# The gate of the state-space layer: from VectorE, behind its scaled inputs, to GpSimd, behind its seventh addition

## The reference

```python
def _ssm(x, W_in, conv_w, dt_bias, A_log, D, norm_w, W_out):
    zxbcdt = x @ W_in.T
    z, xBC, dt_raw = ...                       # 512, 768 and 64 columns
    xBC = _causal_conv_silu(xBC, conv_w)       # -> xs, B, C
    dt = jax.nn.softplus(dt_raw + dt_bias)
    a = dt * -jnp.exp(A_log);  cum = jnp.cumsum(a)
    M = (C B^T) * exp(cum_i - cum_j), lower triangle, * dt_j
    y = M @ xs + D * xs                        # 128 positions x 512
    yz = y * (z * jax.nn.sigmoid(z))           # the gate
    yn = yz * jax.lax.rsqrt(jnp.mean(yz * yz, axis=-1) + EPS) * norm_w
    return yn @ W_out.T
```

## Time and profile before

| | |
|---|---|
| median of 3 runs | 2140.99 us (2137.66 to 2142.30) |
| the profiled execution | 2138.0 us, of which the span of the profile is 2136.1 |
| busy: TensorE, its weight loads | 1969.5 us (92% of the span), 1276.6 (60%) |
| busy: VectorE, ScalarE, GpSimd | 1627.4 (76%), 1378.5 (65%), 1230.6 (58%) |
| chain that ended last | PE 64%, DVE 16%, issue 7%, ACT 7%, POOL 5% |
| mean granted TensorE clock | 0.978 of full speed |

### The profile page before, as it was taken

One profiled execution on the slowest core, in us unless ns is written; L12 is line 12 of the kernel. 1 busy time (PEld: TensorE's weight loads), 2 busy tenths in 40 slices (PEclk: granted clock), 3 DMA queues, 4 the chain that ended last, 5 costly groups with the idle time before them and its releaser, 6 DMA issues.

```text
span 2136.1 us, 34822 instructions
## 1 busy us (share of the span) xinstructions
PE 1969.5 (92%) x9518; PEld 1276.6 (60%) x9620; DVE 1627.4 (76%) x3852; ACT 1378.5 (65%) x5262; POOL 1230.6 (58%) x1508
## 2 busy tenths in 40 slices
PE   7979999999999998799998848999999999999996
PEld 4636666666666666455554425666666666666664
DVE  7845676766776667689999846788888888787887
ACT  3555666666666666456663237777777777777774
POOL 0153445445545443377777825777777777777774
PEclk9989999999999999999999969999999999999999
DMA  6000000000000002100010020000000000000000
GB/s 229 1 18 6 3 4 3 2 2 5 2 2 2 2 0 85 69 1 30 21 31 10 1 74 16 4 4 6 6 6 6 6 8 6 6 5 6 3 3 8
DMA packets 30235, 37.56 MB, mean 18 GB/s; under 512 B 3472, under 2 KB 24464, under 8 KB 29456
## 3 DMA queue, kind: packets, MB, share of 16 engines
q1 hardware_dynamic: 30096, 36.11, 5.0%
HBM read 34.01 MB, written 2.10 MB: 17 GB/s over the span
## 4 chain that ended last, share of the span: by engine, by line
PE 64%; DVE 16%; issue 7%; ACT 7%; POOL 5%; DMA 0%; DVEq 0%; SPq 0%; POOLq 0%; ACTq 0%
PE xa_pS L755 5%; PE xa_pJB L736 5%; PE xa_pO L830 5%; PE xa_pY L867 5%; PE fa_pJB L1989 5%; PE xa_pJA L736 4%; PE fa_pS L2071 3%; PE ssm_pX L1434 3%; PE ssm_pL L1428 3%; PE fa_pO L2014 3%; PE fa_pY L2028 3%; PE fa_pJA L1969 2%; PE fa_pH L2120 2%; PE xa_pP L747 2%; POOL fa_rs L1919 2%
## 5 line engine op out<-in xcount | busy, mean ns | idle before, releaser
L2146 ACT ACTIVATE fa_qT<-fa_pH,all_fa_head_vec 128x512 f32<-128x512 f32 x128 | 99.6, 778 | 176.0 <-PE fa_pH L2120 176.0
L1919 POOL TENSOR_TENSOR fa_rs<-fa_rs,all_minus_half 128x4 f32<-128x4 f32 x192 | 197.9, 1031 | 15.0
L2155 ACT ACTIVATE fa_pS<-fa_pS,fa_nb 128x128 f32<-128x128 f32 x512 | 183.2, 394 | 6.8 <-issue 6.8
L1380 POOL TENSOR_TENSOR ssm_y<-ssm_y,ssm_term 128x512 f32<-128x512 f32 x112 | 145.8, 1302 | 60.9 <-DVE ssm_term L1677 39.6
L1916 POOL TENSOR_TENSOR fa_rs<-fa_ms,all_eps5w 128x4 f32<-128x4 f32 x192 | 44.4, 231 | 226.3 <-ACT fa_q_junk L2139 126.2
L2071 PEld LDWEIGHTS fa_pS<-fa_kT,fa_qT 128*128 128x128 f32 x1024 | 124.2, 191 | 65.5 <-ACT fa_qT L2146 58.6
L1944 POOL TENSOR_TENSOR fa_cat<-fa_ov,fa_om 128x512 bf16<-128x512 f32 x125 | 150.5, 1204 | 5.1
L2071 PE MATMUL fa_pS<-fa_kT,fa_qT 128*128 128x128 f32 x1024 | 148.2, 288 | 2.8 <-ACT fa_qT L2146 0.9
L1935 POOL TENSOR_TENSOR fa_ov<-fa_ob,fa_om 128x512 f32<-128x512 bf16 x125 | 144.4, 1156 | 0.9 <-DVE fa_om L2287 0.9
L682 POOL TENSOR_TENSOR xa_rs<-xa_ms,all_eps 128x4 f32<-128x4 f32 (+1 forms) x65 | 13.2, 203 | 225.1 <-ACT xa_junk L906 225.1
L924 ACT ACTIVATE xa_pr<-xa_pS,xa_nb,xa_rs 128x256 f32<-128x256 f32 x256 | 142.5, 568 | 0.2
(11 more groups left out here) (338 smaller groups left out, 5744.9 us busy)
## 6 DMA issues: line engine op xcount, KB each, us to landing
all_shared_weights<-in_fa_w SPq DMA_DIRECT2D x12, 512.0 KB, 3.7
fa_cat<-in_fa_wproj SPq DMA_DIRECT2D x8, 512.0 KB, 3.8
all_shared_weights<-in_xa_wq SPq DMA_DIRECT2D x1, 2048.0 KB, 13.8
xa_wo<-in_xa_wo SPq DMA_DIRECT2D x1, 2048.0 KB, 18.0
xa_ctxT<-in_ctxT SPq DMA_DIRECT2D x16, 128.0 KB, 2.1
all_shared_weights<-in_fa_wkvx SPq DMA_DIRECT2D x1, 2048.0 KB, 9.9
fa_ctxT<-in_ctxT SPq DMA_DIRECT2D x16, 128.0 KB, 2.1
out_x<-all_X SPq DMA_DIRECT2D x16, 128.0 KB, 1.7
```

The costliest lines, as they stand in the source:

```text
L1919: pool.tensor_tensor(rs[:, j % 2, cols], rs[:, j % 2, cols], env.mhalf[:, cols], ALU.pow)\
L2155: last = act.activation(four(pS[j % 2])[:, i, :], four(pS[j % 2])[:, i, :], ACT.Exp, bias=nb[:, j % 2, i:i + 1], accum_out=rsum[:, j % 2, ...
```

## The change

The gate moves from VectorE's list to GpSimd's. GpSimd now multiplies `y` of sequence m by `sz` in step m, right behind the seventh addition, and ahead of its scaled inputs for sequence m + 1. Before, VectorE did it in step m + 1, behind its own scaled inputs for sequence m + 1 (and behind the biased dt, in even steps). It waits for the seventh addition and for `sz`; TensorE's transposes and ScalarE's squares wait for the same semaphore (`gated`) as before.

```diff
@@ gpsimd, steps(m, ...), in "if attend:", behind the loop over the levels
                     if l == 2 and m > 2:
                         norm.pool_rstd(pool, m - 2, 0)
+                pool.wait_ge(y_added, now(m, 0, LEVELS, LEVELS - 1))
+                pool.wait_ge(s["z_in"], now(m, 0))
+                pool.tensor_tensor(y[:, side, :], y[:, side, :], sz[:, side, :], ALU.mult).then_inc(s["gated"], 1)
             elif back:
@@ vector, steps(m, ...)
             if paired and not first:
                 biased_dt(dve, m + 1)
-            if back:
-                dve.wait_ge(y_added, now(m - 1, 0, LEVELS, LEVELS - 1))
-                dve.tensor_tensor(y[:, 1 - side, :], y[:, 1 - side, :], sz[:, 1 - side, :], ALU.mult)\
-                    .then_inc(s["gated"], 1)
             terms(0, 1)
```

## The result

| | before | after |
|---|---|---|
| median of 5 runs | 2140.99 us (2137.66 to 2142.53) | 2150.35 us (2146.87 to 2152.52) |
| span of the profiled execution | 2136.1 us | 2145.1 us |
| first xdt of the stage to the last transpose | 341.8 us | 350.5 us |

The ratio is 1.0045, 95% interval 1.0033 to 1.0057: slower by 0.45%; between the medians lie 9.4 us, against 8.5 forecast. Of the 9.0 us between the two spans 8.7 lie in the state-space stage. Of all the executions reported here one, of the filled kernel before, took 7800.83 us; no profile shows why, and it is left out of that kernel's ratio.

A forecast was written before the change was run, and what follows sets the result against it. Bound: at even entries the path over VectorE's xdt and L1270, with GpSimd holding VectorE up. Pair costs, clock losses and the end sum to 8.7 us, taken as 8.5 over 2141.0: 2149.5 us, range 2139.5 to 2158.

The forecast's parts named there:

- The held xdt: VectorE's xdt, issued 0.18 us into GpSimd's gate, ends 0.55 us behind it: about 1.6 us in place of 0.68.
- Rival 1: At the entries xdt gets through unheld: even ones gain some 0.75 us, 6 us less in all, 2135; chance 0.08.
- The even entry, +0.2: Start of an even step: level 0 starts 0.96 us later, but the step loses 0.2 us at full clock.
- The odd entry, +0.34: Start of an odd step: GpSimd's scaled inputs end later, so y's first part (L1690) ends 0.34 us later.
- Rival 2: VectorE, rid of its gate, makes good the delay before the step's end: about +1.5 us, 2142.5; chance 0.2.
- Rival 3: Behind xdt GpSimd's scaled input starts before VectorE's, adding 1.07 us per entry: 15 more, about 2165; chance 0.03.
- The clock: Even entries: four pairs with lowered clock cost 1.0 us each; 1.5 more lose it, at 1.97 us each.
- The end, +0.4: Step 17: GpSimd's gate takes 1.27 us in place of 0.68, so the transposes start about 0.4 us later.
- L103: not held: The tiny operation ahead of xdt is not held by GpSimd; were it held, 3 us more.
- Rival 4: All even entries lose the clock (3.5 us more, chance 0.1), or L103 is held (3 us, chance 0.04): 2153 to 2156.
- The sum: State-space stage: 4 x 1.0 + 1.5 x 1.97 + 2.5 x 0.54 + 0.4 = 8.7 us, taken as 8.5.

The follow-up runs named there:

- the filled kernel before: Kernel before, with extra matmuls, results dropped, in TensorE's idle time before level 0 of even steps 4 to 14: 2135.43 us beside 2138.22, ratio 0.9988.
- The gate behind xdt: Changed kernel, but GpSimd's gate also waits for VectorE's xdt of the next sequence: 2144.25 us beside 2138.80, ratio 1.0025.
- the added product: Kernel before, VectorE's gate kept but waiting for an extra GpSimd product y times sz at the change's place, result unread: 2154.01 us beside 2138.80, ratio 1.0069.
- the memset: Changed kernel with GpSimd's gate replaced by a memset of both halves of y: 2137.50 us, ratio 0.9993 to the kernel before.
- the filled kernels: Kernels before and after, each with dropped matmuls in TensorE's idle time at even steps 4 to 14: 2135.43 and 2141.71 us, ratios 0.9988 and 1.0017.
- no gate: Kernel before without VectorE's gate, y left ungated: 2137.87 us beside 2138.80, ratio 0.9996; with TensorE's idle time filled too, 2135.08 beside 2140.48, ratio 0.9971.
- the run with the gate first: Kernel before with VectorE's gate ahead of its biased dt in even steps: 2135.47 us beside 2138.22, ratio 0.9988.

## Why the prediction was right, point by point

**The held xdt: right.** Gate 0.08 us behind the addition, 1.27 us, xdt 0.18 us into it and out 0.54 behind it; all as forecast. The gate behind xdt, the added product and the memset show that it is GpSimd's running product that holds xdt, and that a write of the same buffer does not. Rival 1 is out.

One link was read wrong, without harm to the sum. I wrote that xdt follows GpSimd's last addition. It does not wait for it: at step 3 it started at 934.37, inside an addition that ended at 935.20. Xdt stands behind VectorE's own norm, and the first operation of that norm, L112, is itself held by the last but one addition. Here it is before at step 8, and at the stage's end with GpSimd idle:

```profile
1038.76 1.05 DVE L112 TENSOR_SCALAR all_X<-ssm_res,ssm_mean_var,ssm_rstd 128x256 f32<-128x256 f32 x1
...
1233.11 0.41 DVE L112 TENSOR_SCALAR all_X<-ssm_res,ssm_mean_var,ssm_rstd 128x256 f32<-128x256 f32 x1 [0.44 <-POOL ssm_rstd L107]
```

The first meets the addition that began at 1038.39. With 1.27 us that ends at 1039.66, and L112 0.15 behind it, at 1039.81. It took 1.04 or 1.05 us at all 13 entries of steps 4 to 16. So xdt and the end of the last addition are both timed from the addition before it, and lie 0.26 us apart before and after.

**The even entry, +0.2: right.** At full clock it is 21.98 us across the even entry against 21.81. **The odd entry, +0.34: right**, 20.45 against 20.10 (both from the filled kernels). At step 6 y's first part ends 0.55 behind GpSimd's third scaled input, as worked out (1001.08 + 5.29 = 1006.37, and 1006.92). Together +0.52 per pair against 0.54. Rival 2, that VectorE makes the delay good, is out: it would have left the pair at 41.9 to 42.0. Rival 3 is out as well: VectorE's L1270 still starts first, 1001.03 to 1001.08.

**The clock: right in size per pair, by a count that was luck.** Here a pair runs from the end of y's first part one step ahead of the even entry to the one behind it. Where the clock fell before and after, at step 12, it cost 1.00 us more (43.84 against 42.84), against 1.0 forecast. The three pairs that newly have a fall (steps 4, 8 and 10) cost 1.85, 1.99 and 2.20, against 1.97. But step 6, which fell before, did not fall after (its pair became 0.43 cheaper), with 3.19 us of idle time where 2.25 had been enough. Which entries lose the clock was not predicted by anything I read, and stays open: with no gate, step 4 fell at 1.63 us. I took 1.5 more falls and there were 2 in all, three new and one gone. That longer idling brings more of them is borne out by all twelve profiled executions together. At the entries of steps 6 to 12 the clock fell in none of 20 where TensorE had been idle for 0.52 to 0.63 us, in 9 of 20 at 2.22 to 2.26, and in 7 of 8 at 3.19 to 3.21. And after's ratio fell from 1.0045 to 1.0017 when it was filled.

**The end, +0.4: right,** 0.39 more between the seventh addition's end and the gate's. **L103: not held,** 0.15 us inside the gate. That goes for its one element per partition only: L112, a `tensor_scalar` of 256 elements per partition, is held, as shown above. Rival 4 is out in both parts: step 6 kept the clock.

**The sum: 8.7 us for the stage, and 8.7 measured, but the match is luck.** The terms moved against each other:

| | forecast | measured |
|---|---|---|
| the four entries that fell before (6, 12, 14, 16) | 4 x 1.0 = 4.0 | 2.2 |
| entries that newly fall | 1.5 x 1.97 = 3.0 | 6.0 (three) |
| entries at full clock in both | 2.5 x 0.54 = 1.35 | 0.1 (step 2 alone) |
| the end | 0.4 | 0.3 |

The prices per pair held, the counts did not, and the sum changes with the entries that fall. Step 2 cost next to nothing as its xdt was held before too (1.36 us, and 1.37 after).

What I did not have is why VectorE's gate cost anything at all. I put 0.56 us of TensorE's wait in its account; the run with the gate first took that wait away and gave 0.14 per pair. The gate's price, 0.78 per pair, lay in y's first part coming later: from the start of xdt to its end at step 8 it is 7.38 us before and 6.61 without a gate. The sum was unharmed since it was worked out from that part (L1690) and not from the transposes.

Two versions beat both kernels: before with VectorE's gate first, and before with TensorE's idle time filled, each by 0.12%, their intervals just below 1. That is less than the 0.2% taken here as what can be told from no change, so the gain is likely and not sure.

## What to carry to other kernels

Before moving an elementwise operation from VectorE to a GpSimd that idles, look at what VectorE issues in the window where it will run. If that is an operation with two SBUF inputs and on the path, it ended here 0.54 us behind GpSimd's operation, 0.94 us late, and that is paid on VectorE, where the moved work no longer stands. An idle wait of TensorE may be worth little if the step closes over other engines: measure from one fixed point of a step to the next, not by the wait.

## What was not expected of the hardware

- A `tensor_scalar` of 128x256 took 1.05 us beside a GpSimd addition and 0.41 alone; one of 128x1 took 0.15 inside one.
- A GpSimd memset of 0.95 us left VectorE's two-input operation at 0.68 us inside it.
- A held VectorE operation gets in between two queued GpSimd instructions (it ended 0.55 us behind the second of three); it need not wait for the queue.
- Matmuls without use, 2.74 us in a gap of 3.2 us, and two to six at each other even entry from step 4 to 14, kept the granted clock at 1.00 over 220 us. By the ratios (1.0045 and 1.0017, measured apart) that gave after 6 us of 2150; before gained 2.8.
- Idle time alone did not tell where the clock falls: 3.19 us left it at 1.00 at one entry, 2.25 and 1.63 lowered it at others.
